# Feed-forward up projection: seven of a pair's eleven feature tiles by seven block products instead of six

## The reference

```
xq   = fake_quant(layernorm(x))                      # 8 x 1024 rows, 512 wide
gate = einsum('bsh,ih->bsi', xq, quant(w_gate))      # 512 -> 1408
up   = einsum('bsh,ih->bsi', xq, quant(w_up))        # 512 -> 1408
h    = fake_quant(silu(gate) * up)
x    = x + einsum('bsi,hi->bsh', h, quant(w_down))   # 1408 -> 512
```

## Time and profile before

| | before |
|---|---|
| median of 3 runs | 1240.74 us (1240.09 to 1242.16) |
| profiled execution | 1241.54 us, its span 1239.70 us |
| PE busy | 1230.9 us, 99% of the span |
| DVE, ACT, POOL busy | 1052.5 (85%), 858.3 (69%), 384.1 us (31%) |
| stretch of the six pairs, 825.00 to 1041.35 us | 216.35 us: PE 214.05, DVE 193.04, ACT 175.49, POOL 93.43 us busy |

### The profile page before, as it was taken

One profiled execution on the slowest core, in us unless ns is written; L12 is line 12 of the kernel. 1 busy time (PEld: TensorE's weight loads), 2 busy tenths in 40 slices (PEclk: granted clock), 3 DMA queues, 4 the chain that ended last, 5 costly groups with the idle time before them and its releaser, 6 DMA issues.

```text
span 1239.7 us, 20617 instructions
## 1 busy us (share of the span) xinstructions
PE 1230.9 (99%) x7500; PEld 572.3 (46%) x7500; DVE 1052.5 (85%) x1917; ACT 858.3 (69%) x1349; POOL 384.1 (31%) x295
## 2 busy tenths in 40 slices
PE   9999999999999999999999999999999999999998
PEld 5544444444444444444444444544444444444444
DVE  8977988988898898898898869888998998888777
ACT  7888567657757756765775763468888886399760
POOL 0113343144034124314404420224444443022223
PEclk9999999999999999999999999999999999999999
DMA  8384346255354363462562383498777764199996
GB/s 314 90 254 168 94 137 213 69 170 171 95 181 133 113 211 85 119 222 69 159 214 92 107 244 113 166 266 265 235 237 237 271 186 159 43 374 410 425 426 264
DMA packets 174565, 241.74 MB, mean 195 GB/s; under 512 B 122608, under 2 KB 142080, under 8 KB 156928
## 3 DMA queue, kind: packets, MB, share of 16 engines
q1 hardware_dynamic: 174432, 240.42, 58.7%
q10 hardware_dynamic: 32, 0.01, 0.0%
HBM read 120.86 MB, written 90.57 MB: 171 GB/s over the span
## 4 chain that ended last, share of the span: by engine, by line
PE 91%; DVE 3%; ACT 3%; issue 1%; SPq 1%; DMA 1%; POOL 0%; DVEq 0%; POOLq 0%; ACTq 0%
PE bank L2492 12%; PE po L81 10%; PE po L82 9%; PE po L83 9%; PE ring L81 8%; PE ring L82 8%; PE ring L83 8%; PE bank L2369 8%; PE bank L2374 4%; PE bank L2375 4%; PE bank L2350 2%; PE bank L2331 2%; PE ring L1257 2%; PE ring L1284 2%; SPq L1703 1%
## 5 line engine op out<-in xcount | busy, mean ns | idle before, releaser
L81 PE MATMUL ring<-yT,M 128*128 128x512 f16 x512 | 194.3, 379 | 0.0
L83 PE MATMUL ring<-yT,M 128*128 128x512 f16 x512 | 194.2, 379 | 0.0
L82 PE MATMUL ring<-yT,M 128*128 128x512 f16 x512 | 194.2, 379 | 0.0
L81 PE MATMUL po<-VW,p 128*128 128x512 f16 x480 | 182.4, 380 | 0.0
L83 PE MATMUL po<-VW,p 128*128 128x512 f16 x480 | 182.1, 379 | 0.0
L82 PE MATMUL po<-VW,p 128*128 128x512 f16 x480 | 182.1, 379 | 0.0
L494 ACT ACTIVATE p<-E 128x512 f16<-128x512 f32 x120 | 74.6, 623 | 122.9 <-DVE E L741 122.8
L414 POOL TENSOR_TENSOR esum<-E 128x512 f32<-128x512 f32 x16 | 23.4, 1460 | 409.2 <-DVE p L745 369.6
L417 POOL TENSOR_TENSOR esum<-esum,E 128x512 f32<-128x512 f32 x96 | 129.5, 1349 | 51.2 <-ACT E L483 18.4
L2492 PE MATMUL bank<-w,hb 128*128 128x512 f16 x605 | 131.3, 379 | 0.0
L1984 ACT ACTIVATE hb<-hb,hscale 128x512 int8<-128x512 f32 (+1 forms) x155 | 95.2, 705 | 17.5 <-DMA hb<-hidden 14.2
(11 more groups left out here) (389 smaller groups left out, 2495.5 us busy)
## 6 DMA issues: line engine op xcount, KB each, us to landing
xa<-x_rows_d SPq DMA_DIRECT2D x28, 1024.0 KB, 7.0
hidden<-hb SPq DMA_DIRECT2D x22, 1024.0 KB, 10.1
hb<-hidden SPq DMA_DIRECT2D x18, 1024.0 KB, 10.6
x<-in_x_dram SPq DMA_DIRECT2D x16, 1024.0 KB, 5.3
value_fold<-E SPq DMA_DIRECT2D x64, 256.0 KB, 2.5
VW<-value_fold SPq DMA_DIRECT2D x16, 1024.0 KB, 6.5
x_rows_d<-x SPq DMA_DIRECT2D x16, 1024.0 KB, 5.1
out_dram<-xa SPq DMA_DIRECT2D x11, 1024.0 KB, 12.2
```

What stands on the lines that cost most here:

```text
L81: nc.tensor.matmul(out, a_hi, b_hi, start=first, stop=False)
L82: nc.tensor.matmul(out, a_hi, b_lo, start=False, stop=False)
L83: return nc.tensor.matmul(out, a_lo, b_hi, start=False, stop=last)
```

## The change

Joint tiles become 0, 2, 3, 5, 6, 8 and 9, single ones 1, 4, 7 and 10. A single tile's first-group half stands behind the joint tile ahead of it, its second-group half with the joint tile that follows; tile 10's second half moves into the next pair's first stretch. The first product of a joint tile that has a joint tile in front of it is issued ahead, in that tile's stretch (`ahead`).

```diff
-    JOINT = tuple(range(0, FT, 2))
+    JOINT = tuple(i for i in range(FT) if i % 3 != 1)
+    SINGLE = tuple(i for i in range(FT) if i % 3 == 1)
...
+    ahead = lambda i: i > 0 and i - 1 in JOINT
...
-            nc.gpsimd.tensor_tensor(wsum[:, 2], every(wg, 0), every(wu, 0), ALU.subtract).then_inc(w_summed, 1)
-            nc.gpsimd.tensor_tensor(wsum[:, 0], every(wu, 0), every(wu, 2), ALU.add).then_inc(w_summed, 1)
+            for n in range(2):
+                nc.gpsimd.tensor_tensor(of_them(2, n), third_tiles(wg, 0, n), third_tiles(wu, 0, n), ALU.subtract).then_inc(w_summed, 1)
+                nc.gpsimd.tensor_tensor(of_them(0, n), third_tiles(wu, 0, n), third_tiles(wu, 2, n), ALU.add).then_inc(w_summed, 1)
...
         for p in PAIRS:
+            early = {5: (2 * p + 3, 3)}
+            late = {2: (2 * p + 3, 1), 3: (2 * p + 3, 2), 6: (2 * p + 4, 0), 8: (2 * p + 4, 1), 9: (2 * p + 4, 2)}
+            if p == 1:
+                early[2] = (2 * p + 3, 0)
+            else:
+                early[0], late[0] = (2 * p + 2, 3), (2 * p + 3, 0)
             for i in JOINT:
                 seed(p, i)
                 keep_third(p, i)
...
-                g, t = {2: (2 * p + 3, 0), 4: (2 * p + 3, 2), 6: (2 * p + 4, 0), 8: (2 * p + 4, 2)}.get(i, (NG, 0))
-                if g < NG:
-                    normalise_row(g, t)
+                if i in early and early[i][0] < NG:
+                    normalise_row(*early[i])
                 joint_silu_a(p, i)
-                if i < JOINT[-1]:
+                if i + 1 in SINGLE:
                     single_silu(p, i + 1, 0)
-                if g < NG:
-                    normalise_row(g, t + 1)
+                if i in late and late[i][0] < NG:
+                    normalise_row(*late[i])
                 keep_fourth(p, i)
...
             for i in JOINT:
...
+                begins = i + 1 in SINGLE
+                if not ahead(i):
                     joint_first(p, i)
                 joint_third(p, i)
...
+                if half_made:
+                    single_product(*half_made, 2)
                 if i > 0:
-                    single_product(p, i - 1, 2)
-                if joint(p, i) > 0:
-                    joint_close(p if i > 0 else p - 1, i - 2 if i > 0 else JOINT[-1])
-                if 0 < i < JOINT[-1]:
-                    single_product(p, i - 1, 3)
+                    joint_close(p, JOINT[JOINT.index(i) - 1])
+                elif p - 1 in PAIRS:
+                    joint_close(p - 1, JOINT[-1])
+                if half_made and begins:
+                    single_product(*half_made, 3)
                 joint_middle(p, i)
-                if i < JOINT[-1]:
+                if begins:
                     single_product(p, i + 1, 0)
                     single_product(p, i + 1, 1)
                 else:
-                    single_product(p, i - 1, 3)
-                    if p + 1 in PAIRS:
-                        pe.wait_ge(x_turned[0], 64 * (p + 1))
-                        joint_first(p + 1, 0)
+                    single_product(*half_made, 3)
+                    joint_first(p, i + 1)
                 joint_late(p, i)
```

More of the change, by code:

```diff
@@ L1519, in order_of_products @@
         for K in range(ALL_J):
-            if K == 0 or K % NJ:
+            if not ahead(JOINT[K % NJ]):
                 made.append(("first", K))
@@ L1525, in order_of_products @@
             made += [("second", K), ("gate_a", K)]
-            if K % NJ == NJ - 1 and K + 1 < ALL_J:
+            if ahead(JOINT[(K + 1) % NJ]):
                 made.append(("first", K + 1))
@@ L1540, in taken_joint @@
         return len(TAKEN) * K + k + (k >= 2) if K > 0 else k + 1
-    single = lambda p, i: NS * (p - 1) + i // 2
+    single = lambda p, i: NS * (p - 1) + SINGLE.index(i)
     wide_w = w[:, 0:2].rearrange("p j n -> p (j n)")
@@ L1700, in turn @@
             elif g // 2 > 2:
-                sp.wait_ge(joints, made_joint("gate_b", joint(g // 2 - 2, JOINT[-1])))
+                sp.wait_ge(singles, 4 * NS * (g // 2 - 2))
             for t in range(TT):
@@ L1710, in store_h @@
                 p = g // 2
-                sp.wait_ge(single_hs, 2 * (single(p, m1 // 2 * 2 - 1) + 1))
-                sp.wait_ge((j_hs_a, j_hs_b)[g % 2], joint(p, (m1 - 1) // 2 * 2) + 1)
+                sp.wait_ge(single_hs, 2 * (single(p, max(i for i in SINGLE if i < m1)) + 1))
+                sp.wait_ge((j_hs_a, j_hs_b)[g % 2], joint(p, max(i for i in JOINT if i < m1)) + 1)
             sp.dma_start(h_d[g][:, m0:m1], hb[:, HOME[g], m0:m1]).then_inc(h_stored[HOME[g]][c], 16)
@@ L1767, in on_sync @@
         load_r(ODD)
-        sp.wait_ge(joints, made_joint("gate_b", ALL_J - 1))
+        sp.wait_ge(singles, 4 * ALL_S)
         load_r(1)
@@ L1820, in sum_weights @@
             pool.wait_ge(x_rounded, 1)
-            every = lambda half, c0: half.rearrange("p c (i n) -> p c i n", n=P)[:, c0:c0 + 2, 0:FT:2]
-            nc.gpsimd.tensor_tensor(wsum[:, 2], every(wg, 0), every(wu, 0), ALU.subtract).then_inc(w_summed, 1)
-            nc.gpsimd.tensor_tensor(wsum[:, 0], every(wu, 0), every(wu, 2), ALU.add).then_inc(w_summed, 1)
-            pool.wait_ge(x_rounded, 2)
[L1825 to L1828, removed]
+            third_tiles = lambda half, c0, n: half.rearrange("p c (i n) -> p c i n", n=P)[:, c0:c0 + 2, 2 * n:FT:3]
+            of_them = lambda k, n: wsum[:, k, :, n:len(JOINT):2]
+            for n in range(2):
+                nc.gpsimd.tensor_tensor(of_them(2, n), third_tiles(wg, 0, n), third_tiles(wu, 0, n), ALU.subtract).then_inc(w_summed, 1)
+                nc.gpsimd.tensor_tensor(of_them(0, n), third_tiles(wu, 0, n), third_tiles(wu, 2, n), ALU.add).then_inc(w_summed, 1)
+            pool.wait_ge(x_rounded, 2)
+            for n in range(2):
+                pool.wait_ge(w_summed, 2 * n + 2 if n == 0 else 4)
+                nc.gpsimd.tensor_tensor(of_them(1, n), of_them(0, n), third_tiles(wg, 0, n), ALU.subtract).then_inc(w_summed, 1)
+            for n in range(2):
+                pool.wait_ge(w_summed, 5 + n)
+                nc.gpsimd.tensor_tensor(of_them(3, n), third_tiles(wg, 2, n), of_them(1, n), ALU.subtract).then_inc(w_summed, 1)
         def add_fourth(p, i):
@@ L1959, in on_scalar @@
                 keep_third(p, i)
+                if i == 0 and p - 1 in PAIRS:
+                    single_silu(p - 1, SINGLE[-1], 1)
+                elif i - 1 in SINGLE:
+                    single_silu(p, i - 1, 1)
                 if i > 0:
-                    single_silu(p, i - 1, 1)
-                if joint(p, i) > 0:
-                    joint_silu_b(p if i > 0 else p - 1, i - 2 if i > 0 else JOINT[-1])
-                g, t = {2: (2 * p + 3, 0), 4: (2 * p + 3, 2), 6: (2 * p + 4, 0), 8: (2 * p + 4, 2)}.get(i, (NG, 0))
-                if g < NG:
-                    normalise_row(g, t)
+                    joint_silu_b(p, JOINT[JOINT.index(i) - 1])
+                elif p - 1 in PAIRS:
+                    joint_silu_b(p - 1, JOINT[-1])
+                if i in early and early[i][0] < NG:
+                    normalise_row(*early[i])
                 joint_silu_a(p, i)
-                if i < JOINT[-1]:
+                if i + 1 in SINGLE:
                     single_silu(p, i + 1, 0)
-                if g < NG:
-                    normalise_row(g, t + 1)
+                if i in late and late[i][0] < NG:
+                    normalise_row(*late[i])
                 keep_fourth(p, i)
+        single_silu(PAIRS[-1], SINGLE[-1], 1)
+        joint_silu_b(PAIRS[-1], JOINT[-1])
         for n in range(2 * FT, 4 * FT):
             silu(n)
-            if n == 2 * FT:
-                joint_silu_b(PAIRS[-1], JOINT[-1])
         act.wait_ge(scales_ready, 3)
@@ L2143, in on_vector @@
         for p in PAIRS:
[L2144 to L2150, removed]
             single_hidden(p, 1, 0)
@@ L2155, in on_vector @@
                 pair_reach(p - 1, 8)
[L2156 removed]
             cross(p, 2)
             if p - 1 in PAIRS:
[L2159 to L2160 removed]
+                pair_reach(p - 1, 9)
             else:
@@ L2164, in on_vector @@
                 join_group(1)
-            single_hidden(p, 3, 0)
+            single_hidden(p, 1, 1)
             joint_hidden_a(p, 2)
+            if p - 1 in PAIRS:
+                pair_reach(p - 1, 10)
+                join_pair(p - 1)
+            cross(p, 3)
             pair_reach(p, 1)
+            single_hidden(p, 4, 0)
+            joint_hidden_a(p, 3)
             pair_reach(p, 0)
-            single_hidden(p, 3, 1)
-            cross(p, 4)
-            pair_reach(p, 3)
+            cross(p, 5)
             round_x(2 * p + 3)
-            single_hidden(p, 5, 0)
-            joint_hidden_a(p, 4)
+            single_hidden(p, 4, 1)
+            joint_hidden_a(p, 5)
             pair_reach(p, 2)
-            single_hidden(p, 5, 1)
             cross(p, 6)
-            pair_reach(p, 5)
+            pair_reach(p, 4)
             single_hidden(p, 7, 0)
             joint_hidden_a(p, 6)
```

(44 more changed lines are left out.)

13 lines of the change are left out of this document (6 added, 7 removed).

## The result

The changed kernel takes 1248.17 us (median of 6, 1247.88 to 1249.11) against 1240.79 us (median of 6): ratio 1.006, 95% interval 1.005 to 1.007, 7.4 us slower. I had forecast 1239.7 us and a range from 1237.4 to 1244.3.

A forecast was written before the change was run, and what follows sets the result against it. TensorE was taken to set the pair stage's time, 0.2158 us per matmul. The terms -2.59 + 1.75 + 0.14 + 1.9 + 0.25 - 2.4 gave -1.0 us, from 1240.74 to 1239.7 us, range 1237.4 to 1244.3.

The forecast's parts named there:

- What is removed: TensorE, pair stage: one more block-product tile per pair removes 12 matmuls in all, -2.59 us.
- The short slot's own gap: 20-matmul stretches between fourth products: second product waits 0.135 us for ScalarE's seed copy, three times a pair; +1.75 us.
- ScalarE kept up: ScalarE's 18 extra instructions fit with nothing to spare; only pair 1's tile 2 is late, +0.14 us once.
- Tile 2's cross sum: VectorE, pairs 2 to 6: behind a 1.89 us even rounding and a reduction, late by 0.38 us; +1.9 us.
- What is given back: TensorE's two long waits, blamed on input sums standing where transposed input lands late, both go: -2.4 us.
- The odd rounding, tiles 6 and 0: VectorE: rounding held by GpSimd's product to about 1.8 us, yet cross sums of tiles 6 and 0 cost nothing.
- Tile 9: VectorE: input sums meet GpSimd's add, making this tile's cross sum 0.05 us late five times; +0.25 us.
- Rival (c): VectorE behind GpSimd becomes the bound, tiles 6, 9 and 0 each 0.3 us later: +4.4, 1245.1 us; chance 0.22.
- the full hold: Even rounding at tile 2 starting only after GpSimd's add, ending 0.14 us later: 0.7 us more; not adopted.

The follow-up runs named there:

- e7: Kernel before the change, with a reduction in front of the first two next-pair input sums and the last two behind tile 8's cross sum: 1239.14 us, ratio 0.9992.
- e8: Changed kernel with VectorE's order mended around the cross sums of tiles 2, 3 and 9, second timing: 1238.12 us, ratio 0.9984.
- e3: Changed kernel with GpSimd's add cut to 8 of 512 columns and its product replaced by a zero fill, VectorE's list untouched: 1238.32 us, ratio 0.9983.
- e5: Changed kernel with tile 2's cross sum directly behind the even rounding, in front of both reductions of the pair before: 1246.41 us, ratio 1.0050.

## Why the prediction was wrong

- **What is removed**: right. 12 matmuls fewer; e7 against e8 gives 0.74 us for them net of the short slot's gaps.
- **The short slot's own gap**: right, 18 gaps of 0.135 us, also with the GpSimd work gone (e3). ScalarE kept up in every slot but pair 1's tile 2, which costs the 0.14 us that I had given it.
- **Tile 2's cross sum**: right, five waits of 0.36 us for 0.38, and e5 takes them away.
- **What is given back**: the waits are gone as forecast, 2.4 us by the traces, but their cause was only half told. "They come from one thing", the late input, leaves out that the third sum of 1.64 us was held by GpSimd's product until 0.55 us behind its end; by its 0.68 us elsewhere, that is 0.96 of the 1.27 us of the first wait (an estimate). Lateness and hold came together. And e7, which takes both waits away, gains 1.1 us in its median, so in most executions the kernel before may lose less to them than in the profiled one; no second trace of it is there to show it.
- **Not in the sum**: a gap of 0.35 us at the start of the stretch, in the profiled execution of before, is absent after the change. It is absent in e7 too, whose code there is that of before, so it is a difference between executions.
- **The odd rounding, tiles 6 and 0**: right. GpSimd's product begins 0.60 to 0.65 us ahead of the rounding, which takes 1.70 to 1.75 us for 1.8, and no cross sum there is waited for.
- **Tile 9, the step that failed**: "the second starts 0.47 behind the add's end, at 2.83, and the cross sum of tile 9 [...] at 2.83 + 0.61 = 3.44, late by 0.05". The start at 2.83 is right (894.49 - 891.65 = 2.84). But I let the second sum run free. By my own count for the short slot the second silu is at M+1.90, so GpSimd's product is at 1.90 + 0.69 + 0.13 = 2.72, 0.11 ahead of the sum. It holds the sum to M+4.59. Waits of 1.1 us instead of 0.05: 5.3 us of the miss. I had used exactly that product for the odd rounding and not here.
- **Tile 3, the step left out**: I priced the join nowhere; alone it takes 0.17 us. It has two inputs in SBUF and stands where that same product runs, and so costs the rest of the product: 5 x 0.53 = 2.7 us.
- Rival (c) was the right mechanism, at 0.22, and I sized it wrongly: it is no spread of 0.3 us over three places but whole holds of 0.5 to 1.1 us at two, one of them not on its list.
- On the shared ports, the Trainium skill, "SBUF — State Buffer", "Who interferes with whom", names a VectorE instruction with two SBUF inputs beside the conversion, against a GpSimd instruction that reads SBUF. I had weighed the conversion's half alone. In this case the traces agree with the other half: join and sums are held (0.90 and 1.75 us), the reduction (at most 1.21) and the cross sum (one input in PSUM, at most 0.70) never are, and in e3 the join is 0.17 us long while GpSimd fills with zeros. For the rounding, the row's 1.89 us held and not the full hold that I had set beside it: tile 2's waits are 0.36 us, not 0.52.

The terms as measured in the traces: -2.6 matmuls, +1.9 short gaps (pair 1's included), +1.8 tile 2, +5.6 tile 9, +2.7 tile 3, -2.4 long waits, -0.4 the gap at the start, and small differences that, with rounding, bring it to +6.4 us, of 6.6 between the spans. The medians differ by 7.4; the profiled execution of before lies 0.75 above its median, that of after at it.

## What to carry to other kernels

When a hand-written order shortens the distance between two deadlines, put the other engine's instructions on the same time line for every instruction in front of the deadline, not for the long ones: in these traces, what a VectorE instruction takes beside GpSimd is set by its inputs and by when GpSimd began, and 11 elements can take 0.9 us. Order such instructions behind the one that is waited for, and put in front of it one that is not held up. A held instruction shows as busy, with no idle time ahead of it; compare the minimum and the maximum of its line.

## What the runs showed of the hardware

The join of 128 x 11 takes 0.17 us alone, 0.90 when GpSimd's product has 0.87 us left, and 0.36 when it has 0.34 left (e5). The sums end 0.55 us behind GpSimd's end and take 0.68 alone; the rounding ends 1.08 behind it and takes 1.22 alone. So both end about 0.14 us earlier than GpSimd's end plus their own time.

The hold works both ways. In the kernel before, the odd rounding of the earlier trace rows began first, at 843.48, and kept its 1.23 us; GpSimd's add, 1.27 us long elsewhere, took 1.81:

```profile
844.02 1.81 POOL L1835 TENSOR_TENSOR hb<-hb 128x512 f32<-128x512 f32 x1 [2.31 <-ACT hb L1935]
```
